# A four-layer block on one core: the FFN's turn and products at other half steps, SP's spread in four calls, two weight copies that wait

## The reference

```python
x = x + _layernorm(_L0_attn_ref(_layernorm(x), ...))   # causal attention, 16 heads of 8, relative bias
x = x + _layernorm(_L0_ffn_ref(_layernorm(x), ...))    # silu(x Wg) * (x Wu), then Wd, hidden 384
x = x + _layernorm(_L1_attn_ref(_layernorm(x), ...))   # quaternion attention, 16 heads, normalised q and k
x = x + _layernorm(_L1_ffn_ref(_layernorm(x), ...))    # 8 experts, top 2, gelu, hidden 512
```

## Time and profile before

| | |
|---|---|
| median of 3 runs | 879.85 us (879.59 to 881.98) |
| the profiled execution | 872.1 us, span 869.9 us |
| mean granted clock of PE | 0.947 of full speed |
| PE, DVE, ACT, POOL busy | 736.0, 419.1, 501.3, 180.4 us |
| rounds (start of each, about) | 0, 121.7, 226.6, 371, 511, 643 us; tail from 750 |

### The profile page before, as it was taken

The page is one execution under the profiler, slowest core; times in us unless marked ns, Lnnn a source line. Parts: engine busy times, 40 slices in busy tenths (PEclk is TensorE's granted clock), DMA queues, the critical chain, the costliest instruction groups (busy, mean ns, idle before and its releaser), DMA issues. The chain is left out here.

```text
span 869.9 us, 21028 instructions
## 1 busy us (share of the span) xinstructions
PE 736.0 (85%) x8160; PEld 522.1 (60%) x8160; DVE 419.1 (48%) x1389; ACT 501.3 (58%) x1030; POOL 180.4 (21%) x307
## 2 busy tenths in 40 slices
PE   4779997989779999888989987887786878789994
PEld 3668775768545667665555753455553656467763
DVE  3355426664253464225353566473866646531236
ACT  3456564586557586866658765558454556543231
POOL 7101010000100000010100005132315287036230
PEclk9999998999889999999999999999887999989997
DMA  4610400002400000511000412000511021101010
GB/s 113 204 15 3 152 7 5 5 2 64 126 4 14 17 2 15 149 29 17 4 15 1 127 46 72 19 22 22 165 46 43 26 80 37 33 26 50 19 40 24
DMA packets 72358, 40.43 MB, mean 46 GB/s; under 512 B 42726, under 2 KB 62140, under 8 KB 72132
## 3 DMA queue, kind: packets, MB, share of 16 engines
q1 hardware_dynamic: 70468, 35.81, 15.1%
q0 software_dynamic: 1536, 3.15, 1.2%
q10 hardware_dynamic: 256, 0.13, 0.1%
HBM read 20.98 MB, written 17.96 MB: 45 GB/s over the span
## 5 line engine op out<-in xcount | busy, mean ns | idle before, releaser
L954 ACT ACTIVATE late<-ps,j_bias 128x512 f32<-128x512 f32 x256 | 173.9, 695 | 136.3 <-PE ps L1768 135.4
L1220 DVE TENSOR_REDUCE neg_max<-ps 128x2 f32<-128x32 f32 (+31 forms) x128 | 90.5, 707 | 188.3 <-PE ps L1612 179.7
L1768 PE MATMUL ps<-q_heads,k_parts 128*128 128x512 f32 x256 | 131.6, 531 | 20.8 <-ACT late L954 17.2
L794 ACT ACTIVATE probsT<-ps 128x128 f32<-128x128 f32 (+3 forms) x271 | 102.8, 429 | 76.7 <-PE ps L1627 50.0
L880 ACT ACTIVATE probs<-ps,neg_max 128x16 f32<-128x16 f32 (+31 forms) x256 | 110.5, 494 | 16.7 <-DVE neg_max L1220 16.3
L1627 PE MATMUL ps<-ident,probs 128*128 128x128 f32 x640 | 97.1, 283 | 7.5 <-ACT probs L880 7.5
L664 POOL TENSOR_TENSOR q_wide<-qT,eighth_mask 128x1024 f32<-128x1024 f32 x16 | 31.3, 1954 | 303.2 <-PE ps L1612 175.9
L1627 PEld LDWEIGHTS ps<-ident,probs 128*128 128x128 f32 x640 | 76.8, 144 | 26.7 <-ACT probs L880 10.7
L1768 PEld LDWEIGHTS ps<-q_heads,k_parts 128*128 128x128 f32 x256 | 48.5, 197 | 68.9 <-ACT late L954 46.7
L1783 PE MATMUL ps<-late,v_two 128*9 128x512 f32 x512 | 71.3, 630 | 10.9 <-DVE late L1206 8.7
L1605 PE MATMUL ps<-kT_two,q_wide 64*64 64x262 f32 (+16 forms) x1024 | 74.8, 357 | 4.4 <-ACT probsT L794 2.7
(11 more groups left out here) (271 smaller groups left out, 1166.3 us busy)
## 6 DMA issues: line engine op xcount, KB each, us to landing
k_parts<-k_half SPq DMA_DIRECT2D x16, 256.0 KB, 3.1
q_parts<-q_half SPq DMA_DIRECT2D x16, 256.0 KB, 3.9
k_parts<-k_parts SPq DMA_DIRECT2D x16, 256.0 KB, 3.3
q_heads<-q_parts SPq DMA_DIRECT2D x64, 64.0 KB, 2.2
x_by_expert<-q_heads SPq DMA_DIRECT2D x3, 960.0 KB, 7.7
probsT<-x_by_expert SPq DMA_DIRECT2D x45, 64.0 KB, 1.9
y_by_expert<-probsT SPq DMA_DIRECT2D x45, 64.0 KB, 1.5
q_rel<-q_by_token SPq DMA_DIRECT2D x128, 8.0 KB, 2.4
```

Of the source, the lines that this page charges most:

```text
L794: return nc.scalar.activation(o, i, ACT.Copy)
L954: nc.scalar.activation(head_probs[:, i % SLOTS, :], ps[:, banks[i % len(banks)], :], ACT.Exp, bias=j_bias[:]).then_inc(e2_ready.sem, 1)
L1220: nc.vector.tensor_reduce(neg_max[:, n % 4, :], ps[:, k:k + OCT, 0:QS * (n + 1)], axis=AXX, op=ALU.max, negate=True).then_inc(max_ready.se ...
L1768: mm(ps[:, banks[i % R], :], k_parts[:, hg, kc * P:(kc + 1) * P], q_heads[:, hg % 2, g, :], start=True, stop=True).then_inc(s2_ready.sem, 1)
```

## The change

In the second to fourth round the FFN's pieces 5 and 6 go three half steps later (11 and 12 become 14 and 15, in the fourth round 13 and 14 become 16 and 17). Pieces 7 to 23 start at half step 18 instead of 19 in the fourth round and stay in the second and third, since `late // 2` is 1 and 0. SP's `spread` is cut into four calls in place of two. POOL's copies of tiles 2 and 3 of the second and third expert batch (b = 1 and 2) wait for PE's transposition of tiles 0 and 1 of their batch.

```diff
-                put(r, 6 + late, "F", f, 7)
-                put(r, 17 + late, "F", f, 17)
+                put(r, 6 + late, "F", f, 5)
+                put(r, 14 + late, "F", f, 2)
+                put(r, 17 + late // 2, "F", f, 17)
                 put(r, 34 + late, "F", f, 1)
                 put(r, 38 + late, "F", f, 12)
...
-            put(r, 52, "S", f, 1)
-            put(r, SL - 1, "S", f, 1)
+            for slot in (52, 55, 58, SL - 1):
+                put(r, slot, "S", f, 1)
...
                     sp.dma_start(q_dram[b][:, c, :, :], q_half[:, c % 2, :].bitcast(f32)).then_inc(q_out.sem, 16)
+                yield
                 sp.wait_ge(k_out.sem, k_out.at(b + 1, 0))
                 sp.wait_ge(q_out.sem, q_out.at(b + 1, 0))
                 spread_k(b, 0)
                 spread_q(b, 0)
+                yield
                 spread_k(b, 1)
                 spread_k(b, 2)
                 yield
...
                             pool.wait_ge(yx_ready.sem, yx_ready.at(b, j - 3))
+                        if b and 2 <= j < 4:
+                            pool.wait_ge(xT_ps.sem, xT_ps.at(b, j - 1))
                         e = pool.value_load(tile_at[0:1, b, j:j + 1], min_val=0, max_val=NE - 1)
```

## The result

The changed kernel took 869.09 us in the median of four runs (865.79 to 870.85), the kernel before 879.72 (879.44 to 881.98): ratio 0.9869, interval 0.9834 to 0.9905, 10.6 us less. Six more runs of it, in a later group, gave 864.55 (863.10 to 870.84) against 879.39: ratio 0.9841 (0.9811 to 0.9871), 14.8 us less. Forecast were 869.0 and 10.9 us. The total came as worked out. The terms did not: two neighbouring ones gained 5.4 us together where 1.3 were forecast, and one stretch lost 10.6 us in the profile where I had expected nothing.

What follows compares the result with a forecast made beforehand. PE, busy 85% of the span, bounds the kernel through standstills and half clock. Terms 0.7 + 3.6 + 1.7 + 0 + 1.3 + 3.0 + 2.2 - 1.6 = 10.9 us off the 879.85 median give 869.0, range 863.5 to 876.5.

Steps and rivals of the forecast that it cites:

- Third round's turn: FFN's piece 5 three half steps later, ending PE's 3.64 us wait for VectorE's xn: 3.6 us gained (2.0 to 3.9).
- Fourth round's turn: Same move in the fourth round, where PE waited 1.23 us: 1.7 us gained (0.8 to 2.2).
- Second round's turn: Same move where PE waited 5.14 us; PE then waits for maxima and exps: 0.7 us gained (0.2 to 1.5).
- Half step of the products, and the norm: Fourth round: gate, up, down sooner, 0 (-1.9 to +1.9); second norm's 2.52 us wait shortened, 1.3 us gained (0 to 2.5).
- SP's spread: Fifth round: last two expert tiles' loads issued before SP's wait for k_out and q_out: 3.0 us gained (1.5 to 4.7).
- POOL's wait: Weight copies held back from VectorE's small operations: 2.2 us gained in the sixth round (1.0 to 3.2), -1.6 in the tail.
- the 1.5 that I named as a sign: Sign of being right: VectorE's first small operation L1083 under 1.5 us in the sixth round, over 1.5 in the tail.
- the two conditions named in the prediction: GpSimd contends with Vector instructions in a 2-port mode or with two SBUF inputs; held at fullest, tail costs 2.6 us.
- Rival 1: Stalls only change hands, PE waiting for maxima and exps, half clock returning: 3.5 us gained, 876.4; chance 0.20.
- Rival 2: Shorter stalls keep PE at 2.4 GHz: 15 to 20 us gained, 862; chance 0.10.
- Rival 3: Fourth round's half step makes gate and up products wait for tanh and delays maxima: slower, 884; chance 0.05.

Runs made afterwards that it cites:

- second round's turn unmoved: The changed kernel with the second round's norm pieces left where they were, turn moved in the third and fourth round only: 866.33 us, ratio 0.9868 to before.
- the half step alone: The kernel before with only the gate, up and down products half a step sooner in the fourth round: 874.00 us, ratio 0.9945.
- the turn alone: The kernel before with only the sixth and seventh piece of the FFN's norm stage moved to slot 14 in every round: 877.38 us, ratio 0.9991.

## Why the prediction was right, term by term

- **Third round's turn** (3.6): 4.0 to 4.2 in seven of ten profiles that have it, 2.9 to 3.4 in three. Right, by the mechanism given: the waits of PE that took the old one's place are 0.56 to 0.93 us. The half clock still comes, but for less of the time: over 252 to 260 us the mean is 0.79 in the changed kernel and 0.57 in before.
- **Fourth round's turn** (1.7): 1.7 alone, 2.4 in six of nine with the half step, 0.9 in three. Right in the main; with 2.4 the clock is 1.00 throughout (396 to 402 us of the changed kernel), with 0.9 it is 0.72 over the 6 us from 400 (second round's turn unmoved).
- **Second round's turn** (0.7): not to be told from nothing. PE waits for probs as forecast (3.4 us at 137.48 and 1.1 at 140.64), but the clock sets the end: 0.52 from 143 to 147 us, where the first profile of before has 0.92. The bound of 0.2 was too high.
- **Half step of the products, and the norm** (0 and 1.3): the steps that failed, both mis-sized. Together they gain 5.4 at that place in all ten profiles with the half step; by the times 5.4 alone and 6.2 on top of the turn. The norm has 3.4 of them. Its direction was right (the wait of 2.52 became 0.74), but I priced the wait alone and not the half clock behind it, though the earlier trace rows show just that behind two other stalls. The products have 2.0, just over their upper bound of 1.9: the gain of 1.7 came, and of the loss that I set against it only four waits are seen on PE, 0.16, 0.27 and 0.27 of the up products and 0.44 of one scores.
- **SP's spread** (3.0): 3.3 by the times alone, with the forecast next late thing (2.18 us for DVE's copy). In the fifth round itself it is worth 1.4 on average, since the load that I priced was later in the first profile than in the others; that 3.0 and 3.3 agree is in part luck.
- **POOL's wait** (2.2 and -1.6): 3.0 or 2.5 in the sixth round, 1.2 lost in the tail. Both mechanisms show in the traces. In the second profile of the changed kernel the first small operation takes 2.73 us from 656.23, to the end of the second tile's second copy, as worked out, and more than the 1.5 that I named as a sign; in the first it takes 0.17, since the stand at the second row of scatters kept DVE back until the long copies were over. As for the tail, what is slowed is not L1083 (now L1088) but operations behind it, 0.5 us each beside the copies. The Trainium skill (GPSIMD Engine Reference, Specifications) says that GpSimd's SBUF interfaces are shared with VectorE. The 0.47 to 0.52 us beside a copy against 0.17 without agree. Whether one of the two conditions named in the prediction holds for these operations, no profile shows.
- **The stand at the scatters** was in no term. It stands in both kernels, so the difference of medians is free of it up to its spread: +8.8 in before, +10.6 and +9.2 in the changed kernel. Up to 510 us the changed kernel wins 11.3 us in its first profile, where my terms have 7.3; 10.6 for the whole were measured in the first group, 14.8 in the second. The sum hit because terms for the products and the norm that were 4.1 too small stood against losses at the scatters and in the rest that I had at nothing and 1.6. That it came within 0.1 us of the first median is luck.

Rival 1 (the stalls only change hands) is right for the turn taken alone, as far as the times go, and wrong for the whole. Rival 2 (the clock stays up) is right at the norm and in part at the third round; the mean clock rose from 0.947 to 0.959 in the two profiles, yet was 0.951 in the changed kernel's second. Rival 3 (the half step costs) is refuted by the half step alone.

Open: what the turn alone loses in its slower runs; where the spread wins what the fifth round does not show; whether POOL's wait is worth anything in the times; the resource that stops the engines at the scatters, and why one profile of before lacks it.

## What to carry to other kernels

Price a stall with the half clock behind it: read the granted clock in the windows after each wait, and add what PE loses there. Compare a profiled execution's own time with the median of the runs before resting a sum on it; a gap of 8 us in 880 was an event of 9 us that the profile did not have. When several engines end a long wait at the same moment with no releaser among them, look at what the remaining engine was doing: a pause in GpSimd's row of indirect DMAs gave 4.6 and 7.0 us here, by the two ratios of the changed kernel (0.9841 and 0.9869 to 0.9789).

## What the runs showed that was not expected

While GpSimd issued eight indirect DMAs in a row beside dense PE work, VectorE waited 4.6 to 11.9 us and ScalarE up to 14.4, in twelve of thirteen profiles with the row unbroken (1.5 and 4.4 in the one without the stand); a made row of eight near 60 us did the same (7.5 and 9.7). The kernel's second row, in the sixth round, did so on a smaller scale in twelve of fourteen. A single one did not, and the row with a pause of 2 us behind its first left one such wait of 2.2 us. One edit of a half step on PE moved the granted clock of the 4 us behind it from 0.50 to 1.00.
